# Center and variance matmuls of the mixtures from rounded pairs, and a new order of GpSimd's weight splits

## The reference, cut to what matters

```
def _ln_c(v, eps=1e-06):
    m = jnp.mean(v, axis=1, keepdims=True)
    s = jnp.var(v, axis=1, keepdims=True)
    return (v - m) / jnp.sqrt(s + eps)
```

```
for e in range(E):
    h = jax.nn.gelu(xt @ W1[e] + b1[e], approximate=False)
    ye = h @ W2[e] + b2[e]
    out = out + ye * scores[:, e:e + 1]
```

## Time and profile before

| | |
|---|---|
| median of three runs | 395.4 us |
| profiled execution | 396.52 us, of which the span is 394.5 us |
| mean granted TensorE clock in it | 0.996 |
| PE busy | 377.2 us (96% of the span) |
| ACT, DVE, POOL busy | 289.7, 260.5, 156.0 us |

### The profile page before, as it was taken

How to read it: one execution, slowest core, us unless ns; L and a number is a source line. 1 busy time by engine, 2 the same in 40 slices (tenths; PEclk the granted TensorE clock), 3 DMA queues, 4 the chain that set the end, 5 groups by cost and what they waited for, 6 DMA issues and landing times.

```text
span 394.5 us, 5148 instructions
## 1 busy us (share of the span) xinstructions
PE 377.2 (96%) x1664; PEld 274.8 (70%) x1668; DVE 260.5 (66%) x570; ACT 289.7 (73%) x515; POOL 156.0 (40%) x135
## 2 busy tenths in 40 slices
PE   8999989989999999999999999999999999989895
PEld 3688856445567687887877677877777777646784
DVE  0755656965434864785675986649957497676776
ACT  4552445935106778978889889999899998867883
POOL 5413000920298265123575781212133356332235
PEclk9999999999999999999999999999999999989999
DMA  7950000000000136604110031151120012220332
GB/s 252 446 197 1 2 0 0 2 0 0 2 0 0 32 135 212 265 2 133 28 53 0 2 109 28 45 200 49 41 95 28 27 27 82 55 80 1 90 99 82
DMA packets 11019, 28.64 MB, mean 73 GB/s; under 512 B 1246, under 2 KB 2526, under 8 KB 10736
## 3 DMA queue, kind: packets, MB, share of 16 engines
q1 hardware_dynamic: 10992, 28.31, 20.7%
HBM read 27.69 MB, written 0.62 MB: 72 GB/s over the span
## 4 chain that ended last, share of the span: by engine, by line
PE 67%; DVE 14%; ACT 14%; issue 3%; POOLq 0%; POOL 0%; DVEq 0%; ACTq 0%
PE ps L440 17%; PE ps L441 16%; PE ps L442 16%; ACT hidh L1082 4%; ACT ps L1083 4%; PE ps L447 4%; DVE hidl L1449 2%; PE ps L738 2%; PE ps L452 2%; ACT rstd L967 1%; DVE bot L1365 1%; ACT rstd L969 1%; PE ps L463 1%; DVE small L1364 1%; PE ps L541 1%
## 5 line engine op out<-in xcount | busy, mean ns | idle before, releaser
L1449 DVE TENSOR_TENSOR hidl<-ps,hidh 128x512 fp32r<-128x512 f32 x160 | 108.4, 687 | 53.7 <-ACT ps L1083 52.3
L408 POOL TENSOR_TENSOR x<-x,parts 128x512 f32<-128x512 f32 x43 | 55.9, 1301 | 149.2 <-DVE parts L1459 98.2
L440 PE MATMUL ps<-xh,wh_all 128*128 128x512 f32 x160 | 74.8, 468 | 2.2 <-DVE hidl L1449 1.7
L1082 ACT ACTIVATE hidh<-ps,par 128x512 fp32r<-128x512 f32 x96 | 68.1, 709 | 9.3 <-PE ps L442 7.6
L440 PE MATMUL ps<-hidh,wh_all 128*128 128x512 f32 (+1 forms) x162 | 64.5, 398 | 4.1 <-DVE hidl L1449 3.8
L1083 ACT ACTIVATE ps<-ps,par 128x512 f32<-128x512 f32 x96 | 65.4, 681 | 0.0
L441 PE MATMUL ps<-xh,wl_all 128*128 128x512 f32 x160 | 63.6, 397 | 0.0
L441 PE MATMUL ps<-hidh,wl_all 128*128 128x512 f32 (+1 forms) x162 | 63.6, 392 | 0.0
L442 PE MATMUL ps<-xl,wh_all 128*128 128x512 f32 x160 | 63.2, 395 | 0.0
L442 PE MATMUL ps<-hidl,wh_all 128*128 128x512 f32 (+1 forms) x162 | 63.1, 390 | 0.0
L398 POOL TENSOR_TENSOR wl_all<-wa,wh_all 128x512 fp32r<-128x512 f32 x40 | 51.3, 1299 | 3.5
(11 more groups left out here) (254 smaller groups left out, 581.4 us busy)
## 6 DMA issues: line engine op xcount, KB each, us to landing
scores_all<-rows_scratch SPq DMA_DIRECT2D x48, 256.0 KB, 3.4
wa<-in_moe SPq DMA_DIRECT2D x2, 4096.0 KB, 15.6
wa<-in_moe SPq DMA_DIRECT2D x1, 2048.0 KB, 9.2
dft_o<-in_dft_o SPq DMA_DIRECT2D x1, 640.0 KB
w<-in_w_out SPq DMA_DIRECT2D x1, 576.0 KB, 7.8
cst<-in_consts SPq DMA_DIRECT2D x1, 512.5 KB, 6.8
x<-in_x SPq DMA_DIRECT2D x2, 256.0 KB, 3.1
we<-in_w_experts SPq DMA_DIRECT2D x1, 512.0 KB, 8.6
```

Of the source, the lines that this page charges most:

```text
L408: pool.tensor_tensor(half(x, h), half(x, h), parts[:, n % 2, :], ALU.add).then_inc(s["state_added"], 1)
L440: pe.matmul(o, wh, xhi, start=start, stop=False)
L1082: act.activation(hidh[:, n % 2, f, :], sums, func, bias=bias).then_inc(s["hidden_hi_act"], 1)
L1449: dve.tensor_tensor(hidl[:, n % 2, f, :], bank(sums_bank(n, f)), f32(hidh[:, n % 2, f, :]), ALU.subtract).then_inc(s["hidden_lo"], 1)
```

## The change

Eleven of the twenty center and variance matmuls of versions 3 to 7 change: center of (3, 1), (5, 0), (5, 1) and (7, 0) and variance of (3, 1), (4, 0), (5, 0), (4, 1), (5, 1), (6, 0) and (7, 0). POOL first rounds their operand into the half of `xh` that is not in use and subtracts into `xl` (`split_norm`), and PE then makes two rounded passes (high, then low) with rounded constants, instead of one full-float32 matmul. POOL makes these splits in its own order: the constants once, before the units; a state's or a square's split ahead of a given addition. Variance of (3, 1), (5, h) and (7, 0) is moved one chunk later on PE (the argument `between`). The splits of the second layer's eight experts move: number 0 after the addition of unit 9, numbers 1 to 4 after units 12 to 15, numbers 5 and 6 after units 16 and 17, and number 7 after unit 20. The other waits stay as they are.

```diff
--- before.py
+++ after.py
@@ -88,7 +88,7 @@
...
-    "centered", "squared", "variance", "log_var", "rstd", "normed", "norm_hi", "norm_lo",
+    "state_split", "square_split", "centered", "squared", "variance", "log_var", "rstd", "normed", "norm_hi", "norm_lo",
...
@@ -131,6 +131,7 @@
...
+        norm_w = sb("norm_w", [C, 2 * C], F32R)
...
@@ -248,6 +249,9 @@
         def variance_bank(n, h):
             return 2 + h if n < 3 else 7
 
+        state_splits = [(3, 1), (5, 0), (5, 1), (7, 0)]
+        square_splits = [(3, 1), (4, 0), (5, 0), (4, 1), (5, 1), (6, 0), (7, 0)]
+
         def work(t, n, h):
             return half(t, h) if n < 4 else t[:, 0:HALF]
 
@@ -398,6 +402,21 @@
                     last = pool.tensor_tensor(wl_all[:, e, cols], wa[:, e, cols], f32(wh_all[:, e, cols]), ALU.subtract)
                 last.then_inc(s["w_split"], 1)
 
+            def split_norm(h, src, done):
+                pool.tensor_copy(half(xh, h), src)
+                pool.drain()
+                pool.tensor_tensor(half(xl, h), src, f32(half(xh, h)), ALU.subtract).then_inc(done, 1)
+
+            def split_state(n, h):
+                if n > 3:
+                    pool.wait_ge(s["variance"], seq(n - 1, h))
+                x_ready(pool, n, h)
+                split_norm(h, half(x, h), s["state_split"])
+
+            def split_square(n, h):
+                pool.wait_ge(s["squared"], seq(n, h))
+                split_norm(h, work(sq, n, h), s["square_split"])
+
             def add_part(n):
                 h = n // E % 2
                 if ends_half(n):
@@ -415,21 +434,50 @@
             for e in range(EARLY):
                 split_expert(e, 1024)
             pool.wait_ge(s["img_back"], 2)
+            pool.wait_ge(s["norm_consts_loaded"], 16)
+            pool.tensor_copy(norm_w[:], cst[:, 0:2 * C])
             for n in range(E):
                 for e in range(EARLY + 2 * n, min(EARLY + 2 * n + 2, E)):
                     split_expert(e, 1024)
+                if n == 2:
+                    split_state(3, 1)
+                elif n == 3:
+                    split_square(3, 1)
                 add_part(n)
+
+            def split_next(e):
+                pool.wait_ge(s["part_sums"], E + e + 1)
+                split_expert(e, 1024)
+
             pool.wait_ge(s["moe2_loaded"], 16)
-            for n in range(E, 2 * E):
-                add_part(n)
-                pool.wait_ge(s["part_sums"], n + 1)
-                split_expert(n % E, 1024)
-            for n in range(2 * E, 3 * E):
-                add_part(n)
-            for n in range(3 * E, 4 * E):
-                add_part(n)
+            for kb in (1, 2):
+                hh = (kb + 1) % 2
+                for j in range(E):
+                    if j == 0:
+                        split_square(4, hh)
+                    elif j == 2:
+                        split_state(5, hh)
+                    elif j == 3:
+                        split_square(5, hh)
+                    add_part(kb * E + j)
+                    if kb == 1 and j == 1:
+                        split_next(0)
+                    elif kb == 1 and j >= 4:
+                        split_next(j - 3)
+                    elif kb == 2 and j < 2:
+                        split_next(5 + j)
+                    elif kb == 2 and j == 4:
+                        split_next(7)
+            for j in range(E):
+                if j == 0:
+                    split_square(6, 0)
+                elif j == 1:
+                    split_state(7, 0)
+                elif j == 2:
+                    split_square(7, 0)
+                add_part(3 * E + j)
                 pool.wait_ge(s["moe3_loaded"], 16)
-                split_expert(n % E, 512)
+                split_expert(j, 512)
             for n in range(4 * E, UNITS - 1):
                 add_part(n)
 
@@ -443,11 +491,21 @@
 
             def center(n, h):
 
+                if (n, h) in state_splits:
+                    pe.wait_ge(s["state_split"], state_splits.index((n, h)) + 1)
+                    pe.matmul(bank(center_bank(n, h)), norm_w[:, 0:C], half(xh, h), start=True, stop=False)
+                    pe.matmul(bank(center_bank(n, h)), norm_w[:, 0:C], half(xl, h), start=False, stop=True).then_inc(s["centered"], 1)
+                    return
                 x_ready(pe, n, h)
                 pe.matmul(bank(center_bank(n, h)), k("center"), half(x, h), start=True, stop=True).then_inc(s["centered"], 1)
 
             def variance(n, h):
 
+                if (n, h) in square_splits:
+                    pe.wait_ge(s["square_split"], square_splits.index((n, h)) + 1)
+                    pe.matmul(bank(variance_bank(n, h)), norm_w[:, C:2 * C], half(xh, h), start=True, stop=False)
+                    pe.matmul(bank(variance_bank(n, h)), norm_w[:, C:2 * C], half(xl, h), start=False, stop=True).then_inc(s["variance"], 1)
+                    return
                 pe.wait_ge(s["squared"], seq(n, h))
                 pe.matmul(bank(variance_bank(n, h)), k("mean"), work(sq, n, h), start=True, stop=True).then_inc(s["variance"], 1)
 
@@ -809,9 +867,11 @@
                     front(n + 1, (0,))
                     back(n, (0, 1))
 
-            def second_half(n):
+            def second_half(n, between=None):
                 if widths(n) == widths(n + 1):
                     for f in range(widths(n) // 2, widths(n)):
+                        if between and f == widths(n) - 1:
+                            between()
                         front(n + 1, (f,))
                         back(n, (f,))
                 else:
@@ -868,9 +928,7 @@
 
             for j in range(E):
                 first_half(j)
-                if j == 4:
-                    variance(3, 1)
-                elif j == 5:
+                if j == 5:
                     logits(1)
                 elif j == 7:
                     turn_route(1)
@@ -880,6 +938,8 @@
                     turn_route(0)
                     front(1, (3,))
                     back(0, (3,))
+                elif j == 4:
+                    second_half(j, lambda: variance(3, 1))
                 else:
                     second_half(j)
                 if j == 3:
@@ -893,13 +953,14 @@
                     first_half(kb * E + j)
                     if j == 0:
                         center(4, hh)
-                    elif j == 4:
-                        variance(5, hh)
                     elif j == 5:
                         logits(nx)
                     elif j == 7:
                         turn_route(nx)
-                    second_half(kb * E + j)
+                    if j == 4:
+                        second_half(kb * E + j, lambda: variance(5, hh))
+                    else:
+                        second_half(kb * E + j)
                     if j == 0:
                         if kb >= 2:
                             pe.wait_ge(s["rows_ready"], kb + 1)
@@ -915,13 +976,14 @@
                 first_half(3 * E + j)
                 if j == 0:
                     center(6, 0)
-                elif j == 3:
-                    variance(7, 0)
                 elif j == 4:
                     logits(4)
                 elif j == 6:
                     turn_route(4)
-                second_half(3 * E + j)
+                if j == 3:
+                    second_half(3 * E + j, lambda: variance(7, 0))
+                else:
+                    second_half(3 * E + j)
                 if j == 0:
                     pe.wait_ge(s["rows_ready"], 4)
                     variance(6, 0)
```

## The result

The changed kernel takes 403.87 us (median of 6 runs, 403.46 to 406.15), the kernel before 395.33 (6 runs). The ratio is 1.0213 with a 95% interval of 1.0188 to 1.0239: slower by about 2%, with the border of 2% inside the interval. The profiled execution took 403.68 us with a span of 401.8, 7.3 longer than before.

A forecast was written before the change was run, and what follows sets the result against it. PE, 96% busy, was taken to bound the kernel, with ACT stretches between. Terms 0.7 - 0.4 - 0.3 + 1.6 + 2.9 + 0.6 (restarts) + 2.6 (clock) = +7.7 on 395.4 gave 403.1 us, range 397.0 to 406.5.

The forecast's parts named there:

- likeliest case: Whole kernel: three long PE waits for POOL and about two clock falls, 403.1 us, own range 401.8 to 404.6; chance 0.40.
- Center and variance (3, 1): PE waits 1.5 us for POOL's state split at center; variance waits for nothing; two savings make 0.8; net +0.7.
- Variances (4, 0) and (6, 0): At each, PE waits 0.2 us for the square's split and saves 0.4; -0.4 for both.
- POOL in time: Rival for the whole kernel: all waits vanish and the savings stay, 393.1 us; chance 0.09.
- Center and variance (5, 0): POOL is free; ACT's logarithm sets the end and is reached earlier by the faster center; -0.3, between 0 and -0.4.
- Variance (4, 1) and expert 7's split: POOL's queue makes PE wait 2.0 us at variance, net +1.6, and about 3 before unit 23's first front, +2.9.
- The clock: Behind long PE waits the clock falls: 1.7 us after the 2.0 wait, 0.9 after that of 3, nothing after 1.5; +2.6.
- The rival in which the passes are no faster: At the changed matmuls, two rounded passes save nothing, so counted savings of 2.3 us go: 405.4 us; chance 0.04.
- the case of three falls: Clock falls at all three long waits, the last not hidden in its wait: 2.5 us unstated as sum, 405.6 us; chance 0.13.
- DVE held up as well would give as much: Added to the 405.6 us case: POOL's splits also holding up DVE would give the same time.
- What hides the rest: Moved splits of experts 0 to 6, the third layer's load and POOL's later additions are covered by slack: 0.
- The rule that was weighed: Moved splits of experts 5 and 6 would hold up DVE's gated sum by about 1.0 us; not in the forecast sum.

The follow-up runs named there:

- e6: Changed kernel with POOL's splits and PE's waits kept, but one full float32 matmul on the unrounded tile instead of two rounded passes; 403.59 us.
- e5: Changed kernel with expert 7's split and state (3, 1)'s split each one unit earlier, expert 4's split behind the (4, 1) square's; 395.85 us.
- e1: Changed kernel with POOL's split of expert 7's weight issued one unit earlier, after unit 19's addition; 398.86 us.
- e10: e5 with only the seven pairs of squares (variances); all center matmuls full float32 again; 395.81 us.
- e9: e5 with only the four pairs of states (centers); variances full float32 at the places of the kernel before; 395.68 us.
- e2: Changed kernel with expert 4's weight split behind the split of the squared state of (4, 1), no longer ahead of it; 400.74 us.
- e7: Changed kernel without any pairs, the three variances put back; only the second layer's weight splits stay moved; 399.29 us.
- e4: Changed kernel with PE multiplying an unread tile during the waits ahead of variance (4, 1) and unit 23's first front; 400.95 us.
- e11: Kernel before plus two pairs only, the states of (3, 1), split one unit earlier, and of (5, 0); 395.44 us.
- e12: e11 with PE multiplying an unread tile seven times in its 1.61 us wait ahead of center (7, 1)'s unit; 394.76 us.

## Why the prediction was right, and where it was not

403.1 us was forecast and 403.87 measured, within the likeliest case's own range, and by its mechanism: three waits for POOL, and the clock down behind two of them. Step by step, in the steps of the ledger:

| step | forecast | measured |
|---|---|---|
| (3, 1), with a restart of 0.2 | +0.9 | +1.3 |
| (4, 0) | -0.2 | 0.0 |
| (5, 0) | -0.3 | -0.3 |
| variance (4, 1), with 0.2 and a fall of 1.7 | +3.5 | +3.25 |
| expert 7's split with 0.2 and a fall of 0.9; (6, 0) at -0.2 | +3.8 | +4.3 |
| from there to the end | 0 | -1.3 |
| sum | +7.7 | +7.3 |

The last step is no part of the medians' rise of 8.5 us. It comes from the profiled execution of the kernel before, which has a fall of the clock near 350 us and a mean clock of 0.996. In the groups of the experiments the runs of the kernel before with that mean took 396.0 to 396.9 us, those with 0.997 and more 394.3 to 395.8 (but for one of 1288), where the median lies; the prediction took 1.1 off for this. Without the last step the measured ones add up to 8.6, so the forecast was 0.8 too low, for the reasons that follow. That the clock fell twice was in part luck: the prediction had one fall and one stay to go by, and e6, with waits as long, has no fall in its profile.

**Center and variance (3, 1).** The wait was as read: PE was free at 151.26 and started at 152.73, 1.5 later. The two savings of 0.40 were not: the pair took 0.53 from its start to the next pass, a saving of 0.33, and "Variance is a chunk later and POOL is done by then: free" was wrong. PE did not wait for it, but ACT's logarithm did: at (3, 1) in the changed kernel by 0.18 (timeline of ACT), in e5 by 0.45.

```profile
158.13 0.69 ACT L1029 ACTIVATE rstd<-ps,cst 128x512 f32<-128x512 f32 x1 [0.18 <-PE ps L507]
```

**Variances (4, 0) and (6, 0).** The waits are there (0.10 at 184.51 and 0.19 at 298.18), and the forecast saving of 0.4 at each is not, or not in full: B to C is 0.0 here, a gain of 0.13 to 0.17 in e1 to e5, and of 0.03 in e10, which has the squares' pairs alone. These two and the variance of (3, 1) are the mis-sized terms. Rival "POOL in time" carried the same error, 393.1 where e5, which is that case, took 395.85: the savings of 2.3 that it kept are 0.3 in the ledger.

**Center and variance (5, 0)** came out as forecast, -0.3: e9 gains 0.41 there by the state's pair, and e10 loses 0.16 by the square's.

**Variance (4, 1) and expert 7's split** were read from the order of POOL's queue: waits of 1.92 and 2.81 for 2.0 and 3.0, with POOL's split of expert 7 ending at 278.1, 7.1 behind where that front stood; 4.2 of that is the delay that it already had (the prediction carried 1.6 of it to this place and forecast 4.5), so 2.9 are its own, as forecast. e2, e1 and e7 show each cause by itself.

**The clock.** It fell behind two of the three, the forecast's count, and cost 1.6 and 1.5 (forecast 1.7 and 0.9; the slow stretch did not begin within the longer wait but behind it, from 278.6). The fall that the kernel before has in its profile is missing in the changed kernel's: PE still waits 1.61 at that place, now at 357.93, and the clock stayed up there. That is the -1.3. The rival in which the passes are no faster is ruled out by e4 and e6, 2.6 us apart with the clock up in both. In the case of three falls, "DVE held up as well would give as much" does not follow: by the prediction's own 1.0 that is 404.1 and not 405.6.

**What hides the rest** held: of the weight splits PE waited for expert 7's alone, and the third layer's load, issued at 278.15, delayed no one. The rule that was weighed (the Trainium skill, page SBUF — State Buffer, section Who interferes with whom) would have added up to 1.0. The trace shows a hold-up there, but of another instruction than the gated sum: ahead of the gated sum a DVE scaling of 128x2 elements, with one SBUF input and not two, took 0.48 us and ended as POOL's subtraction did, at 256.6 (timelines of DVE and POOL in the changed kernel).

```profile
256.12 0.48 DVE L1632 TENSOR_SCALAR small<-small 128x2 f32<-128x2 f32 x1 [1.41 <-ACT small L1167]
256.63 0.88 DVE L1635 SCALAR_TENSOR_TENSOR x<-xn,small,x 128x256 f32<-128x256 f32 x2
```

```profile
254.06 2.51 POOL L402 TENSOR_TENSOR wl_all<-wa,wh_all 128x512 fp32r<-128x512 f32 x2
```

The same instruction took 0.17 before, at 251.90, so the hold-up was 0.3. Where no wait at (4, 1) shifts it against POOL it was longer, 0.95 in e5 and e9 and 1.02 in e7 (timelines of DVE and POOL):

```profile
251.91 1.02 DVE L1634 TENSOR_SCALAR small<-small 128x2 f32<-128x2 f32 x1 [0.36 <-ACT small L1169]
```

```profile
250.37 2.52 POOL L402 TENSOR_TENSOR wl_all<-wa,wh_all 128x512 fp32r<-128x512 f32 x2
```

So a hold-up of nearly the forecast size is there, but little comes of it: from E to F e5 loses 0.10 and e9 0.01.

## What to carry to other kernels

A cheaper instruction whose operand must first pass through another engine saves only where that engine gets the operand early: the state's pair of (3, 1), ready 7 us before PE wanted it in e11 (143.7 against 151.0), gave its 0.4 us; being early was not always enough, since the pair of (5, 1) in e9, which PE did not wait for either, gave nothing. The squares' pairs gave next to nothing, because 2.0 us of splitting, or the later place in PE's queue that makes room for it, went into a chain that had no slack. When work is moved in an in-order queue, read what the move puts it behind: here one unit's place in POOL's queue was worth 4 us. And look at the clock of each run before two times are compared, since a fall that stays away can hide an effect as large as the one under study.

## What was not expected of the hardware

Behind waits of the same length, ended by the same engine, the granted clock fell in one execution and stayed in another: after 1.92 us at 239.88 in the changed kernel it went to 0.50, after 1.92 us at 239.87 in e1, with the same work ahead, it stayed at 1.00; after 1.61 us it fell in the kernel before and in e11, and not in the changed kernel. Within e1 the mean clock is 0.999 in five executions and 0.995 or 0.996 in five others. The Trainium skill, page TensorE: Matmul & The Clock Gate, section Part 1: The HAM clock gate, says that the number of matmuls run at the low level as a kernel starts differs from run to run; these runs show the like in mid-kernel. With PE kept busy through the wait the clock stayed at 1.00 in all three places where this was tried (e4 twice, e12). What decides without a filling stays open.

A matmul behind a wait also comes slowly into step: from the first pass of a pair to the second are 0.30 to 0.34 us after waits of 0.03 to 1.92 us in the changed kernel, and 0.23 or 0.24 without a wait. Keeping PE busy did not help there: behind the filling in e4, at 239.10, it is 0.34 too.
